# Attention heads of a four-layer recurrent kernel: 56 stacked rows in place of 72, and row halves of the array in place of column quarters

## What is computed

```
scores = q @ k.T * scale          # q, k: 2048 x 8
probs  = softmax(scores)          # layer 3: only keys up to the query
out    = probs @ v                # v: 2048 x 8
```

## Time and profile before

| | |
|---|---|
| median of 3 runs | 1994.11 us (1992.37 to 1998.57) |
| span of the profiled execution | 1923.2 us |
| own time of the profiled execution beside its span | not given apart from the three runs; the median is 70.9 us above the span |
| PE busy | 1697.7 us (88%) |
| DVE busy | 1435.9 us (75%) |
| ACT busy | 1143.8 us (59%) |
| heads of layer 0 | about 56 to 745 us of the span |
| heads of layer 3 | about 1397 to 1851 us of the span |
| mean granted TensorE clock | 0.931 of full speed |

### The profile page before, as it was taken

How to read it: one execution, slowest core, us unless ns; L and a number is a source line. 1 busy time by engine, 2 the same in 40 slices (tenths; PEclk the granted TensorE clock), 3 DMA queues, 4 the chain that set the end, 5 groups by cost and what they waited for, 6 DMA issues and landing times. The chain is left out here.

```text
span 1923.2 us, 44062 instructions
## 1 busy us (share of the span) xinstructions
PE 1697.7 (88%) x17529; PEld 802.7 (42%) x17529; DVE 1435.9 (75%) x2718; ACT 1143.8 (59%) x2262; POOL 307.7 (16%) x460
## 2 busy tenths in 40 slices
PE   3799999999999995889997798892779999999977
PEld 2222222222222222434444544781425555555556
DVE  5889999999999954665555507656779999999735
ACT  3268888888888894332222244452317777777754
POOL 0103000010000100000000345443012232210123
PEclk8789999999999998799997899996759999999988
DMA  4112111121111012033233269861511111111132
GB/s 143 36 30 81 63 55 51 55 81 64 55 51 34 28 28 59 33 66 106 95 89 144 69 225 333 268 186 48 191 33 30 33 37 37 34 36 36 28 76 70
DMA packets 78037, 154.52 MB, mean 80 GB/s; under 512 B 18684, under 2 KB 35964, under 8 KB 74136
## 3 DMA queue, kind: packets, MB, share of 16 engines
q1 hardware_dynamic: 63034, 121.38, 20.0%
q0 software_dynamic: 14384, 29.29, 4.9%
q10 hardware_dynamic: 414, 1.04, 0.2%
HBM read 102.23 MB, written 48.89 MB: 79 GB/s over the span
## 5 line engine op out<-in xcount | busy, mean ns | idle before, releaser
L856 ACT ACTIVATE heads_probs<-heads_pS 128x512 f32<-128x512 f32 (+3 forms) x1664 | 851.6, 573 | 187.9 <-PE heads_pS L725 172.2
L881 DVE TENSOR_REDUCE heads_run_max<-heads_pM 128x1 f32<-128x1024 f32 x512 | 592.6, 1216 | 54.6 <-PE heads_pM L747 53.3
L787 PE MATMUL heads_pO<-heads_probs,heads_vh 128*32 128x512 f32 (+2 forms) x3328 | 438.1, 570 | 3.2 <-ACT heads_probs L856 1.4
L725 PE MATMUL heads_pS<-heads_qs,heads_ks 75*32 75x512 bf16 (+3 forms) x4160 | 392.7, 370 | 3.8 <-ACT heads_probs L856 1.6
L892 DVE TENSOR_REDUCE heads_run_max<-heads_pM 128x1 f32<-128x512 f32 x384 | 246.7, 684 | 17.2 <-PE heads_pM L725 13.7
L725 PE MATMUL heads_pS<-heads_q_first,heads_ks 75*32 75x512 bf16 x2496 | 234.4, 377 | 7.9 <-ACT heads_probs L856 7.4
L725 PEld LDWEIGHTS heads_pS<-heads_qs,heads_ks 75*32 75x32 bf16 x4160 | 117.3, 95 | 171.2 <-issue 81.3
L725 PE MATMUL heads_pM<-heads_ks,heads_qs 72*32 72x512 bf16 (+3 forms) x1600 | 174.6, 359 | 1.1 <-DVE heads_run_max L892 0.5
L889 DVE CUSTOM_DVE_ANT_0 heads_masked_out<-heads_pM,heads_mask_end 128x128 bf16<-128x128 f32 (+3 forms) x256 | 120.7, 485 | 19.5 <-PE heads_pM L725 17.2
L787 PEld LDWEIGHTS heads_pO<-heads_probs,heads_vh 128*32 128x32 f32 x3328 | 106.7, 110 | 53.3 <-issue 7.1
L725 PEld LDWEIGHTS heads_pS<-heads_q_first,heads_ks 75*32 75x32 bf16 x2496 | 71.3, 95 | 122.4 <-ACT heads_probs L856 66.8
(11 more groups left out here) (388 smaller groups left out, 2369.0 us busy)
## 6 DMA issues: line engine op xcount, KB each, us to landing
top_weights<-k_comb_dram SPq DMA_DIRECT2D x128, 128.0 KB, 3.0
second_w<-in_L_W_dram SPq DMA_DIRECT2D x12, 1024.0 KB, 10.8
k_hid_slots_dram<-k_zeros SPq DMA_DIRECT2D x8, 1152.0 KB, 5.0
k_h_slots_dram<-second_work SPq DMA_DIRECT2D x48, 192.0 KB, 3.1
second_work<-k_hid_slots_dram SPq DMA_DIRECT2D x48, 192.0 KB, 4.3
k_parts_dram<-proj_part SPq DMA_DIRECT2D x12, 512.0 KB, 4.1
heads_ks<-k_parts_dram SPq DMA_DIRECT2D x63, 96.0 KB
heads_qs<-k_parts_dram SPq DMA_DIRECT2D x40, 96.0 KB
```

Source lines behind the costliest of these rows:

```text
L725: mm = pe.matmul(out[cols, :], still[:, cols], moving, start=start, stop=stop)
L787: mm = pe.matmul(pO[k * 32:k * 32 + VW, int(second), o:BLK], vh[c][:, t, :], probs[u % 2][:, k * BLK + o:(k + 1) * BLK], start=first_chunk ...
L856: act.activation(probs[u % 2][:, k * BLK + c0 - b * BLK:(k + 1) * BLK], pS[:, slot, 0:c1 - c0], ACT.Exp)\
L881: dve.reduce_max(run_max[:, i, blocks[0][0] // 2:blocks[0][0] // 2 + 1], both.rearrange("p k c -> p (k c)"), AX.X).then_inc(taken, 2)
```

## The change

- Of the nine products two are left out (low by middle and low by low): `PRODUCTS = (3, 3, 1)` gives 7 products in 56 rows; the maximum rows are rows 56 to 58, so 59 rows fit in 64.
- Every stack, in both layers, holds these 59 rows twice, from partition 0 and from partition 64. `qd` and `kd` are gone. A head has 10 loads (4 for q, 6 for k) in place of 14 in layer 0 and 8 in layer 3, and 6 DMAs of maximum rows in place of 3.
- A score is one matmul of 59 rows by 128 columns in one half of the array's rows, a fill one of 56 rows for each bank; `turns` hands out the halves by turns, over both kinds.
- On the diagonal two short matmuls in the same half replace the four: `ident_b` with `neg_below` for 64 of the output rows, `ident_swapped` with `neg_below_swapped` for the other 64. The swapped copies are made by four DVE instructions in `load_constants`.
- Layer 0's fills stand after the first and third chunk in every unit.
- Ones are written by two memsets a stack in place of one. Each queue of `load_first_keys` has one half of the key stack and waits for its memset before its first DMA.

```diff
-STK = PARTS * PARTS * HD
+PRODUCTS = (3, 3, 1)
+STK = sum(PRODUCTS) * HD
+HALF = 64
...
+                dve.tensor_copy(K.ident_swapped[to, :], K.ident[at, :]).then_inc(made, 1)
+                dve.tensor_scalar(K.neg_below_swapped[to, :], masks[at, 1, :], NEG, None, ALU.mult).then_inc(made, 1)
...
+def query_loads(K, h):
+    yield 0, 2 * PARTS * HD, K.parts[0][h].rearrange("a d t -> (a d) t").unsqueeze(0).broadcast_to([2, PARTS * HD, T])
+    yield 2 * PARTS * HD, STK, K.parts[0][h, 0]
+def key_loads(K, h):
+    for part, n in enumerate(PRODUCTS):
+        at = sum(PRODUCTS[:part]) * HD
+        yield at, at + n * HD, K.parts[1][h, part].unsqueeze(0).broadcast_to([n, HD, T])
...
         def load_first_keys(queue, turn):
-            keys = list(load_stacks(0, 0))[1::2]
-            for i in range(turn, len(keys), 2):
-                dst, src, sem = keys[i]
-                if i == len(keys) - 1:
-                    queue.wait_ge(ones_set[0], 1)
-                queue.dma_start(dst, src).then_inc(sem, 16)
+            half = (0, HALF)[turn]
+            queue.wait_ge(ones_set[0], turn + 1)
+            for row, end, src in key_loads(K, 0):
+                queue.dma_start(ks[0][half + row:half + end, :], src).then_inc(stacked[0], 16)
...
             def load_max_rows(c):
-                for a in range(PARTS):
-                    sp.dma_start(qs[c % ROUND][STK + a:STK + a + 1, :]...
+                for row in (STK, HALF + STK):
+                    for a in range(PARTS):
+                        sp.dma_start(qs[c % ROUND][row + a:row + a + 1, :]...
...
+            turns = itertools.cycle((0, HALF))
...
+                for k, (b, w) in enumerate(blocks):
+                    at = next(turns)
+                    rows = slice(at, at + STK)
+                    mm = pe.matmul(pM[:, bank_of(c, j, k), 0:w], qs[c % ROUND][rows, i * P:(i + 1) * P],
+                                   ks[c % ROUND][rows, b * BLK:b * BLK + w], start=True, stop=True)
...
-                mm = by_columns(pS[:, slot, 0:c1 - c0], ks[c % ROUND][0:STK + PARTS, u * P:(u + 1) * P],
-                                qs[c % ROUND][0:STK + PARTS, c0:c1], True, not diag)
+                at = next(turns)
+                rows, mask = slice(at, at + STK + PARTS), slice(at, at + HALF)
+                mm = pe.matmul(pS[:, slot, 0:c1 - c0], ks[c % ROUND][rows, u * P:(u + 1) * P],
+                               qs[c % ROUND][rows, c0:c1], start=True, stop=not diag)
                 if diag:
-                    mm = by_columns(pS[:, slot, 0:P], K.ident_b[:, :], K.neg_below[:, :], False, True)
+                    pe.matmul(pS[:, slot, 0:P], K.ident_b[mask, :], K.neg_below[mask, :], start=False, stop=False)
+                    mm = pe.matmul(pS[:, slot, 0:P], K.ident_swapped[mask, :], K.neg_below_swapped[mask, :], start=False,
+                                   stop=True)
...
-                        behind = [(len(new) // 2, 1 + 2 * i)[u % 2] for i in range(len(todo))]
+                        behind = [1 + 2 * i for i in range(len(todo))]
...
-            dve.memset(ks[0][64:96, :], 1.0).then_inc(ones_set[0], 1)
+            for row in (HALF // 2, HALF + HALF // 2):
+                dve.memset(ks[0][row:row + HALF // 2, :], 1.0).then_inc(ones_set[0], 1)
```

More of the change, by code:

```diff
@@ L462, in _ @@
                     dve.tensor_tensor(dst, src, bv.unsqueeze(1).broadcast_to([P, TPB, D]), ALU.add).then_inc(vkept, 1)
-HALF = 64
-PRODUCTS = ((0, 0, 3), (1, 0, 3), (2, 0, 2), (2, 2, 3))
-def first_queries(K, causal):
[L472 to L477, removed]
+def query_loads(K, h):
[5 more added lines that the diff above has]
+        yield at, at + n * HD, K.parts[1][h, part].unsqueeze(0).broadcast_to([n, HD, T])
+def first_queries(K, causal):
+    for half in (0, HALF):
+        for row, end, src in query_loads(K, 0):
+            yield K.first_q[half + row:half + end, :], src
 def causal_plan(causal):
@@ L581, in load_stacks @@
         def load_stacks(p, c):
[L583 to L592, removed]
-        def load_first_keys(queue, turn):
-            keys = list(load_stacks(0, 0))[1::2]
-            for i in range(turn, len(keys), 2):
-                dst, src, sem = keys[i]
-                if i == len(keys) - 1:
-                    queue.wait_ge(ones_set[0], 1)
-                queue.dma_start(dst, src).then_inc(sem, 16)
+            h = ROUND * p + c
+            for half in (0, HALF):
+                for row, end, src in query_loads(K, h):
+                    yield qs[c % ROUND][half + row:half + end, :], src, stacked[c % ROUND]
+                for row, end, src in key_loads(K, h):
+                    yield ks[c % ROUND][half + row:half + end, :], src, stacked[c % ROUND]
+        def load_first_keys(queue, turn):
+            half = (0, HALF)[turn]
+            queue.wait_ge(ones_set[0], turn + 1)
+            for row, end, src in key_loads(K, 0):
+                queue.dma_start(ks[0][half + row:half + end, :], src).then_inc(stacked[0], 16)
         def split_max(queue, g):
@@ L705, in _ @@
             for i in range(1, ROUND):
-                pool.memset(ks[i][64:96, :], 1.0).then_inc(ones_set[i], 1)
-                pool.wait_ge(ones_set[i], 1)
+                for n, row in enumerate((HALF // 2, HALF + HALF // 2)):
+                    pool.memset(ks[i][row:row + HALF // 2, :], 1.0).then_inc(ones_set[i], 1)
+                    pool.wait_ge(ones_set[i], n + 1)
             for i in range(ROUND):
@@ L720, in _ @@
         def _(pe):
-            def by_columns(out, still, moving, start, stop):
-                for g in range(P // VW):
-                    cols = slice(g * VW, (g + 1) * VW)
-                    mm = pe.matmul(out[cols, :], still[:, cols], moving, start=start, stop=stop)
-                return mm
+            turns = itertools.cycle((0, HALF))
             def bank_of(c, j, k):
@@ L2517, in recurrent_layers @@
             K.first_loaded = [nc.alloc_semaphore(f"first_loaded{i}") for i in range(2)]
[L2518 removed]
+            K.first_q = first0.enter_context(nc.sbuf_tensor("heads0_q_first", [P, T], BF16))
             load_constants(nc, K, A)
```

38 lines of the change are left out of this document (14 added, 24 removed).

## The result

The changed kernel takes 2000.63 us (median of 17 runs), the kernel before 1993.07 (17 runs): ratio 1.0041, 95% interval 1.0027 to 1.0055. The forecast was "faster", 1981 us, with 1962 to 1996 as the range of its own case.

What follows compares the result with a forecast made beforehand. PE was taken as the bound, then a loop between ACT and PE, with DVE close. Layer 0's terms sum to -12.7 us, layer 3's to 0: -13 on a 1923.2 span, plus 70.9 around it, 1981 us; range 1962 to 1996.

Steps and rivals of the forecast that it cites:

- Stack loads: Both attention layers: 224 rows a head, asked for a head or more ahead, were forecast to cost nothing.
- Starts: Before the first fills: second memset and more DMA issues, +4.0 us in layer 0 and +3.1 in layer 3.
- Slower: Whole kernel: the outcome of a longer time than before, beyond the 0.3% band; chance 0.27.
- Maximum rows: Six row DMAs a head instead of three: +1 us over layer 0's heads, +9 in layer 3, bounds 3 and 20.
- Heads of layer 0: Layer 0's attention: a head every 38.8 us instead of 40.21, -20 us over 14.4 heads.
- loop: ACT and PE in both layers: sums wait for an exponential, which waits for a score; 2.38 us a unit.
- Heads of layer 3: Layer 3's attention: a head every 25.1 us instead of 26.07, -14 us over 14.7 heads.
- the turn: Per head, time added beyond its units: 0.4 us in both layers.
- the loop and the fills hold each other: Rival, both layers: fills waiting for DVE hold scores, sums and ACT; gain gone, fixed costs stay, 2015 us; chance 0.2.
- Halves at once: Scores and fills: matmuls in both row halves run together, 0.11 us a score; rival says not, about 2045 us, chance 0.08.
- Tails: Last head of each layer, DVE idle: passages lengthen units, +2.8 us in layer 0 and +2.0 in layer 3.
- The clock: PE in the heads: granted clock stays at 1.00, no fall counted; remaining chance 0.02.

Runs made afterwards that it cites:

- a1_spread_loads: The changed kernel with stack loads' outermost dimension eight or more instead of the copy count, 12 loads a head instead of 10: 1985.40 us, 0.9956 of the kernel before.
- a4_start: `a1_spread_loads` with POOL writing the second half's ones and key DMAs of rows without ones not waiting: 1977.87 us, 0.9908 of the kernel before.
- a3_two_row_dmas: `a1_spread_loads` with a head's six maximum rows written by two DMAs of three rows each: 1965.86 us, 0.9851 of the kernel before.
- b1_six_rows: The kernel before with six DMAs of maximum rows a head instead of three, the extra rows read by nothing: 2019.48 us, 1.0118 of the kernel before.
- c2_after_two_rows: The changed kernel, its own loads kept, with six maximum rows written by two DMAs of three rows: 1987.91 us, 0.9938 of the kernel before.
- a6_two_and_start: `a1_spread_loads` with the edits of `a3_two_row_dmas` and `a4_start` together: 1959.37 us, 0.9820 of the kernel before; run again, 1966.33 us, 0.9846.
- b0_before: The kernel before, unedited, run again for a second profile: 1993.08 us.
- b2_one_row_dma: The kernel before with a head's three maximum rows written by one DMA instead of three: 1997.88 us, 0.9985 of the kernel before.
- c3_eight_by_turns: `a6_two_and_start` with eight matmuls in the upper half, then eight in the lower, instead of one by one: 2027.57 us, 1.0131 of the kernel before.
- a2_one_half: `a1_spread_loads` with every score and fill in the upper half of the array's rows: 3100.05 us, 1.5527 of the kernel before.

## Why the prediction was wrong, step by step

- **Stack loads ("I take nothing").** This is the step that failed. It counted rows and bytes, and that later loads are asked for a head ahead. The first head's are not, and "Starts" let them land as they did before: their new outermost dimension left the queries to two engines (share 0.13) and slowed the keys with its three. The change's diff shows it, `broadcast_to([2, ...])` and `[n, HD, T]`. Cost by `a1_spread_loads`: 8.8 us of layer 0's start, 7.2 of layer 3's; ratio 1.0041 without and 0.9956 with spread loads. "Slower" had a chance of 0.27, but for rivals that are not what happened.
- **Starts.** With spread loads they are +5.0 and +7.0 us over before, forecast +3.5 and +3.1. `a4_start` takes off 3.5 and 4.6 of these, so the second memset and the issues behind it cost what the forecast said or somewhat more. What is left of layer 3's +7.0 no run isolates.
- **Maximum rows.** Forecast +1 and +9. Two row DMAs took off 6.4 us in the heads of layer 0 and 8.8 in those of layer 3 (`a1_spread_loads` to `a3_two_row_dmas`). Layer 0 was mis-sized: six issues at 0.61 are 3.7 us, but they last 4.2 to 5.0 in most of its heads, for a reason that no run shows, and PE waits (`b1_six_rows`: +4.6 us there without any other change). In layer 3 the size was right and the place only in part: the 8.8 us lie in the first eight heads, and no regular head pays.
- **Heads of layer 0.** Right: loop 2.38 forecast, 2.39 measured; 38.8 a head with a little for conflicts, 38.62 once the rows are out of the way.
- **Heads of layer 3.** Mis-sized: 25.1 forecast, 25.96 measured, before 26.04, so 1 us of gain in place of 14. The loop is there (2.39 in quiet units), but its fills come in bursts of five to a unit, and two copies stand ahead of DVE's takes. Less the turn's 0.44, the ten units stand 1.71 us over the loop of 23.8, three quarters of it in two units; 0.9 was allowed for that (0.07 a unit, and DVE's 24.0 in place of 23.8). That is the rival "the loop and the fills hold each other" for this layer.
- **Luck in layer 3.** The stage still gains 9.2 us, and that is not the forecast's gain: the seven periods of regular heads give 0.7, the eight of scatter heads 8.5. With two row DMAs the eight take 211.3 to 212.4 us (`c2_after_two_rows`, `a6_two_and_start`, `a3_two_row_dmas`) against 227.9 and 230.3 before (`b0_before`, `b2_one_row_dma`), so some 15 us come there, where none were forecast. On the first profile of before they take 212.8, so there is nothing of the kind to see in the rows that the forecast was made from. No run shows why scatter heads gain.
- **Halves at once.** Right, by 350.90 above and by `c3_eight_by_turns`. (By its own terms that rival's total would be some 2052, not 2045.)
- **Tails.** Right in kind: 45.65 against 41.98 in layer 0, as forecast within 1 us; layer 3's did not show (+0.3 with all that follows, forecast +2.0). No run tried them apart.
- **The clock.** Right for this kernel, 1.00 in both windows; its danger was not seen (`a2_one_half`).
- **The outlier** of 70 us in the shown profile was taken for time around the span. It shifted one term: the scatter heads of layer 3 were read as nearly regular ones (212.8 us for the first eight), where other chips take 227.9.

## What to carry to other kernels

When a change rewrites how a transfer is described, read its outermost dimension: bytes and count can stay while the engines that carry it fall to two. That is free where a load has a head's time (`c2_after_two_rows`, with the slow loads, has heads of 38.62 and 25.95 us all the same) and costs the longer landing where a stage starts. And a loop of measured pieces predicts a period only where the other engine's work is spread as evenly as the loop; find its bursts in the trace before averaging its share, and expect the period to move little until all of them are gone.

## What was not expected of the hardware

- With all scores and fills in one half of the array's rows (`a2_one_half`) the granted clock stood at 0.50 through the heads of both stages, with PE busy 81.00 of 81 us. Both halves by turns, or eight and eight, had 1.00. It fell when the feed-forward steps beside the first fills ended (0.96 from 70 to 80 us, 0.50 after); the kernel before also has 0.50 there, but rises again when the heads begin. The Trainium skill (TensorE: Matmul & The Clock Gate, What's actually happening) says that activity releases the throttle; here a PE without idle time did not release it. No run shows why.
- Three rows written by one DMA cost 0.75 us to issue (median), one row by one 0.59, and six in turn up to 6.56 us in a scatter head: the number of issues, not of bytes, was the cost.
- The same kernel differs by 70 us between chips, 1925.61 and 1994 to 2001. Between the two profiles of before, nearly all of it lies in layers 1 and 2 and in the scatter heads of layer 3.
